# Three shared chunks behind the experts in place of two, in a fused attention and mixture-of-experts kernel

## The chip, the cores and the metric

One core of one Trainium2 chip runs the whole program. The metric is the device time of one execution in microseconds. The core has five engines that run their own instruction streams and meet only at semaphores: PE (matmuls), DVE (vector), ACT (scalar, activations), POOL (GpSimd) and SP, which here only issues DMAs.

## The reference

The input x is 4 sequences of 2048 tokens with 256 features (8192 tokens). Two residual layers follow each other:

```python
x = x + layernorm(attn(layernorm(x)))
x = x + layernorm(ffn(layernorm(x)))
```

`attn` mixes features and not tokens: per sequence and head (16 heads of 16 features), the distances between the rows of x @ Wqk give a 16x16 softmax that is applied to x @ Wv, and Wo follows. So one sequence needs a Gram matrix of x (256x256), a few small matrices made from it, and then one 256x256 matrix that every token is multiplied by.

`ffn` normalizes once more, sends each token to the 2 best of 7 experts (a router Wr, a capacity of 732 places per expert), and adds one shared expert that every token passes:

```python
out = routed + (silu(h @ W1s) * (h @ W3s)) @ W2s      # 256 -> 1024 -> 256
```

## The kernel before

**Groups and chunks.** The 8192 tokens are 16 groups of 512, four in each of four batches (a batch is a sequence). Feed-forward work comes in chunks: one group through the shared expert, or half of one expert's places (14 chunks). Every chunk runs through the same body of `FM` = 8 steps m. In each, PE computes two up projections into two PSUM banks (`up`, 12 matmuls of 512 columns, each product as three of high and low parts), ACT applies silu (L1063), DVE multiplies (L1738), ACT rounds to a high part (L1034), DVE takes the low part (L1714), and three steps later PE does the down projection (`down`, 12 matmuls of 256 columns) into banks 2 and 3. The first half of `up(m+1)` waits for silu of step m, the second half for the DVE multiply of step m. In the last two chunks before the experts, and in all after them, a second pair of banks makes both waits one step looser (`wide`).

**Three phases.** First come `FIRST` = 14 shared chunks with the whole attention and routing woven between them; then the 14 expert chunks; then the `HELD` = 2 shared chunks that were held back, with the final pass woven in.

**Places.** A step m has two places, 2m (behind `up`) and 2m+1 (behind `down` on PE, behind the low part on DVE); place numbers count from the first chunk, so chunk n has places 16n to 16n+15. A table written by hand, `schedule`, says at which place each small step of attention and routing is issued, on every engine that has a part in it. Batch b's steps are set by three origins: `X_AT` (per group q, 4 places apart: `x_stats`, `x_norm`, `x_high` on ACT, `x_part` on DVE, `x_gram` on PE), `M_AT` (the chain of small matrices) and `MIX_AT` (per group, 5 places apart: `o_mix` on PE, `o_stats` and `o_norm` on DVE, `o_apply` on ACT, `o_add`, `u_stats`, `u_norm` on DVE, two turns and the router on PE, `u_copy`). Each pair of groups is then routed: `r_top`, `r_next` on DVE, `u_count` on PE, `u_slot`, `u_place` on DVE. Engines take their streams strictly in order, so a step at place 66 on DVE stands ahead of everything at place 67.

**Waits that the prediction touches.** `x_high` waits for `x_norm`, `x_part` for `x_high`, `x_gram` for `x_part`; `u_count` waits for the second choice made by `r_next` (`r_oh`); `o_apply` waits for `o_norm`, which waits for POOL's power of -0.5.

**The final pass.** Fifteen groups (`GROUP[0..14]`) take the same steps at places `LAST_AT[g]` of the held chunks: DVE statistics (`last_stats`, `last_moments`, L1827 to L1841), a power on POOL (L913), the bias on DVE (L1845), the normalization on ACT in two halves (L1114, at places +3 and +4), and one POOL DMA that adds the group onto the output in DRAM (`last_sum`, L908), three groups later. The groups' expert sums are loaded by SP from `y_scratch` into 13 buffers. The last group (`CLOSE`) is finished from PSUM behind PE's last matmul: DVE adds it in two halves, takes statistics of all four tiles, waits for one power, normalizes, adds the residual and SP stores two halves.

```python
LAST0 = 9
HELD_PLACES = 2 * FM * HELD
LAST_AT = [LAST0 + g * (HELD_PLACES - LAST0 - 4) // (CLOSE - 1) for g in range(CLOSE)]
```

## Time and profile before

| what | value |
|---|---|
| median of 3 runs | 1089.29 us (1087.91 to 1089.88) |
| the profiled execution's own time | 1087.53 us |
| its span, first to last instruction | 1085.8 us |
| mean granted clock of PE | 0.993 |
| busy: PE, DVE, ACT, POOL | 1049.2, 656.1, 503.5, 390.0 us |
| the final pass's first statistics (place 9 of the held chunks) | 1017.77 us |
| DVE's first instruction behind PE's last matmul | 1075.90 us |

The span is what the rows are measured in; 1.7 us lie around it in the profiled execution. PE is busy for 97% of the span, but its busy time is modelled and overlaps from one matmul to the next, so that a group of rows is to be read by its starts. The clock column is the share of full speed (2.4 GHz) that PE was granted in a stretch.

### The profile page before, as it was taken

To read this page: it belongs to the slowest core of one execution; us is meant where nothing else is said; L and a number is where in the kernel's file an instruction comes from. 1 tells how busy PE (TensorE), PEld (TensorE's weight loads), DVE (VectorE), ACT (ScalarE), POOL (GpSimd) and SP (SyncE) were. 2 spreads that over 40 slices of the span, in tenths; PEclk is the share of its full clock that TensorE was granted. 3 is DMA by queue.
4 is the path that set the end of the run, shared out by engine and by line. 5 is a ranking of instruction groups with operands and counts; after the bars stand their busy time and mean duration, and the time that the engine had idled before them with its cause. 6 is when DMAs were issued, how large, how long until landed. Compare 5 with 4: busy or idle time off the path is not lost.

```text
span 1085.8 us, 19513 instructions
## 1 busy us (share of the span) xinstructions
PE 1049.2 (97%) x6863; PEld 958.5 (88%) x6863; DVE 656.1 (60%) x1714; ACT 503.5 (46%) x895; POOL 390.0 (36%) x347
## 2 busy tenths in 40 slices
PE   7998999999999999999989999999999999999995
PEld 6886888888888988889878899999999999999874
DVE  7768864677754578754786334545545463635686
ACT  4343344443434444443454334554546463645485
POOL 3112661114640114541116731344443343312386
PEclk9999999999999999999999999999999999999998
DMA  8322460242540223461134214524344342333699
GB/s 280 114 98 78 138 214 20 78 157 93 174 142 20 100 96 141 134 221 49 59 136 162 93 43 152 139 62 117 82 96 106 68 124 52 81 79 105 239 237 178
DMA packets 47229, 129.15 MB, mean 119 GB/s; under 512 B 10276, under 2 KB 17576, under 8 KB 47152
## 3 DMA queue, kind: packets, MB, share of 16 engines
q1 hardware_dynamic: 28656, 92.83, 25.1%
q0 software_dynamic: 18496, 35.35, 14.2%
q8 instruction: 43, 0.70, 0.3%
q14 instruction: 34, 0.28, 0.1%
HBM read 73.72 MB, written 54.40 MB: 118 GB/s over the span
## 4 chain that ended last, share of the span: by engine, by line
PE 82%; DVE 8%; POOL 3%; issue 3%; ACT 1%; DMA 1%; DVEq 0%; SPq 0%; POOLq 0%; ACTq 0%
PE bank L1140 25%; PE bank L1142 25%; PE bank L1141 25%; PE bank L1159 3%; POOL out_dram L908 2%; POOL sb_place_of L913 2%; DVE sb_act L1738 1%; PE bank L1266 1%; PE bank L1319 1%; DVE sb_act_lo L1714 1%; PE bank L1219 1%; DVE sb_stX L1431 1%; DVE sb_st L1431 1%; PE bank L1278 1%; ACT sb_ln_o L967 1%
## 5 line engine op out<-in xcount | busy, mean ns | idle before, releaser
L1140 PE MATMUL bank<-sb_h_hi,sb_wup_lo 128*128 128x512 f32 (+2 forms) x960 | 354.4, 369 | 5.3 <-DVE sb_act L1738 3.8
L1738 DVE TENSOR_TENSOR sb_act<-bank,sb_act 128x512 f32<-128x512 f32 (+2 forms) x240 | 148.6, 619 | 345.9 <-PE bank L1142 317.1
L1142 PE MATMUL bank<-sb_h_hi,sb_wup_hi 128*128 128x512 f32 (+2 forms) x960 | 350.0, 365 | 0.0
L1141 PE MATMUL bank<-sb_h_lo,sb_wup_hi 128*128 128x512 f32 (+2 forms) x960 | 349.6, 364 | 0.0
L1063 ACT ACTIVATE sb_act<-bank 128x512 f32<-128x512 f32 (+2 forms) x240 | 129.8, 541 | 354.6 <-PE bank L1142 328.9
L1140 PE MATMUL bank<-sb_wdn_hi,sb_act_lo 128*128 128x256 f32 (+1 forms) x848 | 246.5, 291 | 5.8 <-DVE sb_act_lo L1714 5.8
L1142 PE MATMUL bank<-sb_wdn_hi,sb_act_hi 128*128 128x256 f32 (+1 forms) x848 | 240.1, 283 | 0.0
L1141 PE MATMUL bank<-sb_wdn_lo,sb_act_hi 128*128 128x256 f32 (+1 forms) x848 | 239.9, 283 | 0.0
L1140 PEld LDWEIGHTS bank<-sb_h_hi,sb_wup_lo 128*128 128x128 f32 x960 | 180.5, 188 | 27.2 <-DVE sb_act L1738 6.4
L1142 PEld LDWEIGHTS bank<-sb_h_hi,sb_wup_hi 128*128 128x128 f32 x960 | 180.5, 188 | 22.5
L1141 PEld LDWEIGHTS bank<-sb_h_lo,sb_wup_hi 128*128 128x128 f32 x960 | 180.9, 188 | 17.0
L1140 PEld LDWEIGHTS bank<-sb_wdn_hi,sb_act_lo 128*128 128x128 f32 (+1 forms) x848 | 159.7, 188 | 11.6 <-DVE sb_act_lo L1714 6.9
L1714 DVE TENSOR_TENSOR sb_act_lo<-sb_act,sb_act_hi 128x512 fp32r<-128x512 f32 (+2 forms) x240 | 147.2, 613 | 36.1 <-ACT sb_act_hi L1034 34.8
L1141 PEld LDWEIGHTS bank<-sb_wdn_lo,sb_act_hi 128*128 128x128 f32 (+1 forms) x848 | 159.6, 188 | 3.3
L1142 PEld LDWEIGHTS bank<-sb_wdn_hi,sb_act_hi 128*128 128x128 f32 (+1 forms) x848 | 159.5, 188 | 0.0
L1034 ACT ACTIVATE sb_act_hi<-sb_act 128x512 fp32r<-128x512 f32 (+2 forms) x240 | 136.6, 569 | 0.3 <-DVE sb_act L1738 0.3
L864 POOL DMA_INDIRECT y_scratch<-sb_ysb,sb_scur x42 | 76.9, 1832 | 154.1 <-ACT sb_ysb L1052 87.8
L784 POOL TENSOR_TENSOR sb_rstdB<-sb_veB,sb_mhalf 128x4 f32<-128x4 f32 x16 | 19.0, 1187 | 218.1 <-DVE sb_veB L1557 218.1
L800 POOL DMA_INDIRECT sent_scratch<-sb_rows,sb_sendto x64 | 70.7, 1104 | 28.9 <-issue 19.9
L833 POOL DMA_INDIRECT sb_rows<-sent_scratch,sb_gcur x42 | 44.6, 1063 | 77.3 <-issue 52.5
L788 POOL TENSOR_TENSOR sb_rstd<-sb_ve,sb_mhalf 128x4 f32<-128x4 f32 x16 | 19.8, 1239 | 77.5 <-DVE sb_ve L1593 77.5
L967 ACT ACTIVATE sb_ln_o<-bank,sb_nbiasB,sb_rstdB 128x256 f32<-128x256 f32 x64 | 30.9, 563 | 27.5 <-DVE sb_nbiasB L1562 27.5
(265 smaller groups left out, 1240.6 us busy)
## 6 DMA issues: line engine op xcount, KB each, us to landing
sb_xin<-in_L_ffn_W_dram SPq DMA_DIRECT2D x28, 512.0 KB, 3.5
sb_x<-in_L_attn_x_dram SPq DMA_DIRECT2D x16, 512.0 KB, 3.7
out_dram<-sb_x SPq DMA_DIRECT2D x16, 512.0 KB, 3.5
sb_xin<-in_L_attn_x_dram SPq DMA_DIRECT2D x14, 512.0 KB, 5.1
sb_xin<-in_x_turned_dram SPq DMA_DIRECT2D x14, 512.0 KB, 3.9
y_scratch<-sb_ysb SPq DMA_DIRECT2D x14, 512.0 KB, 3.6
sb_xn<-in_L_ffn_W_dram SPq DMA_DIRECT2D x14, 512.0 KB, 3.9
hT_scratch<-sb_hr SPq DMA_DIRECT2D x12, 512.0 KB
```

The lines of the kernel that those rows point to most:

```text
L800: pool.indirect_dma_start(sent_d, bass.IndirectOffsetOnAxis(ap=sendto[:, q, t, c:c + 1], axis=0), u[q][:, t, :], None).then_inc(sent[q], 16)
L833: pool.indirect_dma_start(rows[0:w, part, t, :], None, sent_d, bass.IndirectOffsetOnAxis(ap=gcur[0:w, part, t:t + 1], axis=0)).then_inc(ga ...
L864: pool.indirect_dma_start(y_d, bass.IndirectOffsetOnAxis(ap=scur[0:w, par, part, t:t + 1], axis=0), ysb[0:w, part, t, :], None, compute_op ...
L967: ins = s.activation(ln_o[:, t, :], bank[o_bank(b, q) + t // 2][:, (t % 2) * D:(t % 2 + 1) * D], ACT.Identity, scale=rstdB[:, t:t + 1], bi ...
L1034: s.activation(act_hi[:, m % 4, 0:c.w], act[:, m % 3, 0:c.w], ACT.Copy).then_inc(ahi_ok, 1)
L1063: s.activation(act[:, m % 3, 0:c.w], a[:, 0:c.w], ACT.Silu).then_inc(silu_ok, 1)
L1140: t_.matmul(o, a_lo, b_hi, start=start, stop=False, skip_group_check=True)
L1141: t_.matmul(o, a_hi, b_lo, start=False, stop=False, skip_group_check=True)
L1142: return t_.matmul(o, a_hi, b_hi, start=False, stop=stop, skip_group_check=True)
L1159: ins = t_.matmul(bank[4 + k][:, o:c], a[:, k * P:(k + 1) * P], a[:, o:c], start=(q == 0 and t == 0), stop=(q == GB - 1 and t == GT - 1))
L1714: v.tensor_tensor(act_lo[:, m % 4, 0:c.w], act[:, m % 3, 0:c.w], act_hi[:, m % 4, 0:c.w].bitcast(F32), ALU.subtract).then_inc(alo_ok, 1)
L1738: v.tensor_tensor(act[:, m % 3, 0:c.w], bank[(4 if c.wide and m % 2 else 0) + 1][:, 0:c.w], act[:, m % 3, 0:c.w], ALU.mult).then_inc(act_o ...
```

## The change

`HELD` goes from 2 to 3, so 13 shared chunks stand before the experts and 3 behind them. Four things follow.

1. The woven steps of attention and routing must fit into 208 places, where there were 224. Batch 2 starts 6 places sooner (`X_AT` 66 for 72, `M_AT` 87 for 93, `MIX_AT` 101 for 109), batch 3 starts 16 places sooner (115 for 131, 136 for 152, 148 for 164). Batches 0 and 1 stay. The routing of batch 2 is drawn together: `r_top`, `r_next`, `u_count`, `u_slot` at places 31, 32, 33, 34 behind its origin for its second pair, where they were at 32, 34, 38, 39, and at 21, 21, 22, 23 for the first pair, where they were at 21, 21, 23, 24.
2. Batch 3's first group goes to `hT_scratch` in DRAM and back as the others do (one store and one load of 512 KB more), and 4 more DMAs write zeros into `y_scratch`.
3. The final pass has 48 places. `LAST_AT` runs from 9 to 40 where it ran from 9 to 28. A second group (14) is added from `ysb`; there are 12 buffers; the second last held chunk is loaded behind 11 of the loads.
4. The last group is finished in two halves: each half has its own statistics, moments and power (on POOL), the second is normalized and added to the residual in one DVE operation per tile, and the last `last_sum` stands behind both powers in POOL's stream.

```diff
     TB = N // P
     ST = -(-CAP // P)
     LASTW = CAP - (ST - 1) * P
-    HELD = 2
+    HELD = 3
     FIRST = NG - HELD
...
+
+        def by_memory(b, q):
+
+            return q > 0 or b == B - 1
+
+        def h_stores(b, q):
+            return b * H_LOADS + 16 * sum(by_memory(b, k) for k in range(q))
...
         LAST0 = 9
         CLOSE = NG - 1
         HELD_PLACES = 2 * FM * HELD
-        LAST_AT = [LAST0 + g * (HELD_PLACES - LAST0 - 4) // (CLOSE - 1) for g in range(CLOSE)]
-
-        GROUP = [*range(FIRST - 2), FIRST, FIRST - 2, FIRST - 1, CLOSE]
+        LAST_AT = [LAST0 + g * (HELD_PLACES - LAST0 - 8) // (CLOSE - 1) for g in range(CLOSE)]
+
+        GROUP = [*range(FIRST - 2), FIRST, FIRST - 2, FIRST - 1, FIRST + 1, CLOSE]
...
-                       (0, 1, 3, 3, 4, 4, 5, 6, 8, 8, 11, 12, 13, 13, 14, 14, 15),
+                       (0, 1, 2, 2, 3, 3, 4, 5, 6, 6, 9, 10, 11, 11, 12, 12, 13),
...
-        X_AT, M_AT, MIX_AT = (None, 14, 72, 131), (None, 34, 93, 152), (None, 46, 109, 164)
+        X_AT, M_AT, MIX_AT = (None, 14, 66, 115), (None, 34, 87, 136), (None, 46, 101, 148)
...
-            if b < B - 1:
+            if b == 1:
                 put_routing(b, MIX_AT[b], ((21, 21, 23, 24, 25), (32, 34, 38, 39, 40)), (27, 35, 43, 51), 2)
+            elif b == 2:
+                put_routing(b, MIX_AT[b], ((21, 21, 22, 23, 24), (31, 32, 33, 34, 35)), (26, 33, 40, 47), 2)
             else:
                 put_routing(b, MIX_AT[b], ((21, 21, 24, 25, 26), (31, 31, 34, 34, 35)), (27, 31, 36, 40), 1)
         for j in range(PIECES):
-            put(B - 1, 0, j, [("w_next", 157 if j < 3 else 181 + 2 * j), ("w_high", 182 + 2 * j), ("w_low", 184 + 2 * j)])
-        put(B - 1, 0, 0, [("indices", 200), ("zero_row", 170)])
+            put(B - 1, 0, j, [("w_next", 141 if j < 3 else 165 + 2 * j), ("w_high", 166 + 2 * j), ("w_low", 168 + 2 * j)])
+        put(B - 1, 0, 0, [("indices", 184), ("zero_row", 154)])
...
+            def last_rstd(g, cut, count):
+                pool.wait_ge(t_var, count)
+                v.tensor_tensor(t_scale[g % SLOTS][:, cut], t_ve[g % SLOTS][:, cut], mhalf[:, cut], ALU.pow).then_inc(t_rstd, 1)
+
+            for g in range(CLOSE):
+                last_rstd(g, slice(0, GT), g + 1)
                 if g == 0:
                     pool.wait_ge(t_idx, 1)
                     for k in range(2):
                         pool.wait_ge(x2_out[k], OPEN + 16 * (NG // 2))
                     pool.sem_inc(pool_go, 1)
-                if 3 <= g < CLOSE:
+                if g >= 3:
                     last_sum(g - 3)
-                if g == CLOSE - 1:
-                    for late in range(CLOSE - 3, CLOSE):
-                        last_sum(late)
+            for late in (CLOSE - 3, CLOSE - 2):
+                last_sum(late)
+            for h in range(2):
+                last_rstd(CLOSE, slice(2 * h, 2 * h + 2), NG + h)
+            last_sum(CLOSE - 1)
...
             def last_stats(g):
                 y = last_y[g % TY]
                 dve.wait_ge(t_y[g % TY], 16 * (g // TY + 1))
-                if g == CLOSE:
-                    last_half(g, 0)
-                elif GROUP[g] == FIRST:
-
-                    dve.wait_ge(y_sb, OPEN + NCH - HELD + 1)
-                    v.tensor_tensor(flat4(y), flat4(y), flat4(ysb[:, 0, :, :]), ALU.add).then_inc(t_sum, 1)
-                    dve.wait_ge(t_sum, 1)
+                if GROUP[g] in range(FIRST, CLOSE):
+
+                    h = GROUP[g] - FIRST
+                    dve.wait_ge(y_sb, OPEN + NCH - HELD + h + 1)
+                    v.tensor_tensor(flat4(y), flat4(y), flat4(ysb[:, h, :, :]), ALU.add).then_inc(t_sum, 1)
...
-            for t in range(GT // 2, GT):
-                ins = v.tensor_scalar(y[:, t, :], y[:, t, :], t_scale[CLOSE % SLOTS][:, t:t + 1], t_bias[CLOSE % SLOTS][:, t:t + 1],
-                                      ALU.mult, ALU.add)
-            ins.then_inc(t_sum, 1)
+            y, slot_of = last_y[CLOSE % TY], CLOSE % SLOTS
+            ch = Chain(dve, t_chain, 2 * CLOSE)
+
+            def close_sum(h):
+                dve.wait_ge((dn_half, dn_done)[h], (1, OPEN + NCH * FM)[h])
+                half = flat4(y[:, 2 * h:2 * h + 2, :])
+                v.tensor_tensor(half, half, bank[2 + h][:, :], ALU.add).then_inc(t_sum, 1)
+                dve.wait_ge(t_sum, HELD + h)
+                for t in (2 * h, 2 * h + 1):
+                    ins = v.bn_stats(st[:, t, :], y[:, t, :])
+                ch.link(ins)
+
+            def close_moments(h):
+                for t in (2 * h, 2 * h + 1):
+                    ins = v.bn_aggr(t_mv[slot_of][:, t, :], st[:, t, :])
+                ch.link(ins)
+                cut = slice(2 * h, 2 * h + 2)
+                v.tensor_scalar(t_ve[slot_of][:, cut], t_mv[slot_of][:, cut, 1], EPS, None, ALU.add).then_inc(t_var, 1)
+
+            dve.wait_ge(t_y[CLOSE % TY], 16 * (CLOSE // TY + 1))
+            close_sum(0)
+            close_moments(0)
+            close_sum(1)
+            dve.wait_ge(t_rstd, NG)
+            v.scalar_tensor_tensor(out=t_bias[slot_of][:, 0:2], in0=t_mv[slot_of][:, 0:2, 0], scalar=-1.0,
+                                   in1=t_scale[slot_of][:, 0:2], op0=ALU.mult, op1=ALU.mult).then_inc(t_nb, 1)
+            close_moments(1)
+            for t in (2, 3):
+                ins = v.tensor_scalar(y[:, t, :], y[:, t, :], t_mv[slot_of][:, t, 0:1], None, ALU.subtract)
+            ch.step(ins)
             dve.wait_ge(t_x, 16)
-            for h in (1, 0):
-                dve.wait_ge((t_act, t_sum)[h], (NG, HELD + 2)[h])
-                half = slice(2 * h, 2 * h + 2)
-                v.tensor_tensor(flat4(close_x[:, half, :]), flat4(close_x[:, half, :]), flat4(y[:, half, :]),
-                                ALU.add).then_inc(t_half, 1)
+            dve.wait_ge(t_act, NG)
+            v.tensor_tensor(flat4(close_x[:, 0:2, :]), flat4(close_x[:, 0:2, :]), flat4(y[:, 0:2, :]),
+                            ALU.add).then_inc(t_half, 1)
+            dve.wait_ge(t_rstd, NG + 1)
+            ch.settle()
+            for t in (2, 3):
+                ins = v.scalar_tensor_tensor(out=close_x[:, t, :], in0=y[:, t, :], scalar=t_scale[slot_of][:, t:t + 1],
+                                             in1=close_x[:, t, :], op0=ALU.mult, op1=ALU.add)
+            ins.then_inc(t_half, 1)
```

## Rows read from the trace of the kernel before

**Rows 1.** Busy time by stretch (start:end, length, busy us and count, clock, DMA share, GB/s)
```profile
53.90:644.60 590.70, 579.50 (x3667) 503.91 (x3660) 378.61 (x1043) 251.49 (x419) 206.13 (x186) 0.99 0.33 112
1019.90:1069.00 49.10, 44.59 (x257) 38.63 (x255) 43.39 (x170) 38.44 (x77) 34.10 (x26) 1.00 1.02 263
1069.00:1076.00 7.00, 5.55 (x30) 5.07 (x30) 3.57 (x8) 3.93 (x8) 5.89 (x5) 0.76 1.01 163
```

**Rows 2.** Timeline of PE, last two chunks: start, us, line, idle before, releaser
```profile
1047.50 0.36 PE L1140 MATMUL bank<-sb_wdn_hi,sb_act_lo 128*128 128x256 f32 x1 [2.48 <-DVE sb_act_lo L1714]
...
1067.27 0.38 PE L1140 MATMUL bank<-sb_wdn_hi,sb_act_lo 128*128 128x256 f32 x1 [1.27 <-DVE sb_act_lo L1714]
...
1070.32 0.39 PE L1140 MATMUL bank<-sb_wdn_hi,sb_act_lo 128*128 128x256 f32 x1 [2.08 <-DVE sb_act_lo L1714]
```

**Rows 3.** Timeline of DVE in a chunk with nothing beside it
```profile
615.13 0.69 DVE L1738 TENSOR_TENSOR sb_act<-bank,sb_act 128x512 f32<-128x512 f32 x1 [2.92 <-PE bank L1142]
...
619.35 0.69 DVE L1738 TENSOR_TENSOR sb_act<-bank,sb_act 128x512 f32<-128x512 f32 x1 [2.93 <-PE bank L1142]
```

**Rows 4.** Timeline of DVE in the last pass: one group's start and the next one's
```profile
1051.83 0.75 DVE L1827 BATCH_NORM_STATS2 sb_st<-sb_rows 128x6 f32<-128x256 f32 x2
...
1054.47 0.74 DVE L1827 BATCH_NORM_STATS2 sb_st<-sb_ysb 128x6 f32<-128x256 f32 x2
```

**Rows 5.** Timeline of ACT in the last pass
```profile
1046.30 1.06 ACT L1045 ACTIVATE sb_ysb<-bank 128x512 f32<-128x512 f32 x2
1047.25 2.08 ACT L1114 ACTIVATE sb_x<-sb_x,sb_place_of 128x256 f32<-128x256 f32 x4
```

**Rows 6.** Timeline of DVE at the close
```profile
1075.90 0.69 DVE L1813 TENSOR_TENSOR sb_xn<-sb_xn,bank 128x512 f32<-128x512 f32 x1 [0.93 <-PE bank L1142]
...
1080.30 1.29 DVE L1873 TENSOR_TENSOR sb_rows<-sb_rows,sb_xn 128x512 f32<-128x512 f32 x2
```

**Rows 7.** DMA issues of the end, KB each, median us to landing
```profile
out_dram<-sb_rows SPq DMA_DIRECT2D x2, 256.0 KB, 3.6
...
out_dram<-sb_ysb,sb_outidx POOLq DMA_INDIRECT x1, 6.1
```

**Rows 8.** Timeline of POOL, a power beside DVE and the close's
```profile
1057.60 2.35 POOL L913 TENSOR_TENSOR sb_place_of<-sb_place_of,sb_mhalf 128x4 f32<-128x4 f32 x1
...
1078.19 1.04 POOL L913 TENSOR_TENSOR sb_place_of<-sb_place_of,sb_mhalf 128x4 f32<-128x4 f32 x1 [0.92 <-DVE sb_place_of L1841]
```

**Rows 9.** Timeline of DVE, chunk 8 (places 130 to 137)
```profile
404.84 0.20 DVE L1634 TENSOR_REDUCE sb_best<-sb_lg 128x8 f32<-128x56 f32 x1
...
408.20 1.40 DVE L1431 BATCH_NORM_STATS2 sb_st<-sb_x 128x6 f32<-128x256 f32 x4
...
410.24 1.40 DVE L1431 BATCH_NORM_STATS2 sb_stX<-sb_xin 128x6 f32<-128x256 f32 x4
...
422.85 1.22 DVE L1568 TENSOR_TENSOR sb_wdn_hi<-sb_xn,sb_wdn_hi 128x1024 fp32r<-128x1024 f32 x1
```

**Rows 10.** Timeline of PE, a Gram step of batch 2
```profile
265.80 1.91 PE L1159 MATMUL bank<-sb_wdn_hi 128*128 128x512 f32 x8 [0.32 <-DVE sb_wdn_hi L1568]
```

**Rows 11.** Timeline of ACT before chunk 8: an o_apply
```profile
397.89 1.93 ACT L967 ACTIVATE sb_ln_o<-bank,sb_nbiasB,sb_rstdB 128x256 f32<-128x256 f32 x4 [1.78 <-DVE sb_nbiasB L1562]
```

**Rows 12.** Timeline of DVE, chunk 4 (places 68 to 71)
```profile
240.43 0.22 DVE L1638 TENSOR_TENSOR sb_oh<-sb_same,sb_first 128x56 bf16<-128x56 f32 x1
...
244.86 0.69 DVE L1738 TENSOR_TENSOR sb_act<-bank,sb_act 128x512 f32<-128x512 f32 x1 [0.83 <-PE bank L1142]
...
249.86 0.17 DVE L1680 CAST sb_sendto<-sb_pos 128x16 uint32<-128x16 f32 x1
```

**Rows 13.** Timeline of PE, chunk 4: a count, a turn
```profile
241.17 0.38 PE L1294 MATMUL bank<-sb_oh,sb_earlier 128*128 128x112 bf16 x4
...
251.44 0.60 PE L1266 MATMUL bank<-sb_ident,sb_early 128*128 128x128 f32 x4
```

**Rows 14.** Busy time by stretch, behind a stop of PE in batch 3
```profile
568.00:571.00 3.00, 2.04 (x10) 2.07 (x11) 2.62 (x10) 0.92 (x2) 0.00 (x0) 0.64 0.00 0
```

More of the change, by code:

```diff
@@ L173, in sandwich_kernel @@
         center = ysb[:, 1, 0:KC, :]
-        TY = 13
+        TY = 12
         SLOTS = 5
@@ L179, in sandwich_kernel @@
                   x2[:, 0, :, :], x2[:, 1, :, :], ln_o[:, :, :], by_tile(own[:, 0:GT * D]),
-                  by_tile(rowsf[:, 0:GT * D]), ysb[:, 1, :, :],
+                  by_tile(rowsf[:, 0:GT * D]),
                   hfull[:, :, :].rearrange("p k (t d) -> p (k t) d", d=D)]
@@ L676, in shared_places @@
                 for place in range(2 * FM):
-                    if place == (10 if n == 0 else 2) and j < GB - 1 and n + 1 < FIRST:
-                        load_h(b, j + 1)
+                    if place == (10 if n == 0 else 2) and n + 1 < FIRST and by_memory(*divmod(n + 1, GB)):
+                        load_h(*divmod(n + 1, GB))
                     if place == 2 * BEHIND + 2 and n > 0:
@@ L987, in step @@
                                      scale=gcol[:, 0:1], bias=bcol[:, 0:1]).then_inc(first_hi, 1)
-                    s.activation((hfull if q == 0 else hr)[:, k, :], bank[6 + k][:, :], ACT.Identity,
+                    s.activation((hr if by_memory(b, q) else hfull)[:, k, :], bank[6 + k][:, :], ACT.Identity,
                                  scale=gcol[:, k:k + 1], bias=bcol[:, k:k + 1]).then_inc(hT_ok, 1)
@@ L1008, in prep @@
                         act_e.wait_ge(hf_ok, c.x * 2 + 2)
-                    elif c.held or c.n % GB:
+                    elif c.held or c.loaded:
                         act_e.wait_ge(h_in, c.landed)
@@ L1808, in _ @@
                             ALU.mult).then_inc(t_idx, 1)
-            def last_half(g, h):
-                dve.wait_ge((dn_half, dn_done)[h], (1, OPEN + NCH * FM)[h])
-                half = flat4(last_y[g % TY][:, 2 * h:2 * h + 2, :])
-                v.tensor_tensor(half, half, bank[2 + h][:, :], ALU.add).then_inc(t_sum, 1)
-                dve.wait_ge(t_sum, HELD + h)
             def last_stats(g):
```

34 lines of the change are left out of this document (14 added, 20 removed).

## Prediction

> **What bounds the kernel now.** I read the busy times by stretch first, then PE's timeline for the waits in brackets, then DVE's and ACT's beside them. Of the 590.7 us in which attention is woven into 14 shared chunks, PE is busy for 579.5 [rows 1]; DVE has work for 64% of it. PE is the bound nearly everywhere, and DVE and ACT matter only where they make it stop. They do so in the last pass: the ten steps m from 1019.9 to 1069.0 took 49.1 us [rows 1]. PE stopped there and just behind for 2.48, 1.27 and 2.08 us, each time until DVE's low part was there [rows 2], and the clock stood at 0.76 over 1069 to 1076 [rows 1]. A step with nothing beside it takes 4.21 us [rows 3], so ten would have taken 42.1.
>
> **The held chunks: -7.0 us.** A group of the final pass costs DVE 2.64 us from its statistics to the next group's, of which one low part takes 0.6 [rows 4]: 2.05 us. It costs ACT 2.08 [rows 5]. The pitch is 19 places for 14 groups, at 2.1 us each 2.86 us; that is 72% of DVE, and its own two operations per step (1.2 of 4.21) are 29% more: with the low part of h, over 100%. ACT comes to 73% and 26%. Both fall behind, ACT takes `ysb` late (1.06 us, [rows 5]), and PE waits. After the change the pitch is 31 places for 14 groups, 4.66 us: DVE 44 + 29%, with a 1.2 us low part per chunk and two sums 80%; ACT 45 + 26% and one copy, 75%. The last group ends at place 44 of 48, so nothing of it stands in the last steps. There the last low part needs multiply, high part and low part, about 2.0 us behind `up(7)`; PE has two units of `down` (2.8 us) to do by then. So the 49.1 - 42.1 = 7.0 us go. The clock's share behind it (0.76 over 7 us with 5.55 busy, below 1 us) may go too; I leave it as one bound, -8.0. The other is -5.0, if PE still stops for 1 us at each of the two places where `ysb` is now taken.
>
> **The close: -0.4 us.** I count from DVE's second sum, 1075.90 [rows 6]. Before, the last store can go at 1081.6 [rows 6], lands 3.6 later [rows 7], and the span ends at +9.9. After: sum 0.72, statistics 0.9, bias 0.1, moments and the small add 0.4 give the second half's variance at +2.2; POOL takes it 0.25 later and needs 1.04 [rows 8]: +3.5. DVE's store goes at +4.4 and lands at +8.0. But `last_sum` of group 14 now stands behind that power: it starts at +3.7 and lands 6.1 later [rows 7], at +9.8, and some 0.4 us of waits follow. That row comes from a crowded queue; on an empty one I take 5.3 us, so +9.5. Ends: -1.4 (landing in 4.5) to +0.5 (6.3). The Trainium skill (GPSIMD Engine Reference, Specifications) says that GpSimd's SBUF interfaces are shared with VectorE and contend with DVE instructions that have two SBUF inputs. The trace agrees in kind: a power took 2.35 us beside a busy DVE where it takes 1.04 alone [rows 8]. The change puts the second power beside DVE's subtraction and its final two-input operations, so this rule speaks against it; it is a rival below.
>
> **The woven phase: +12.2 us.** Work is not added, it is pushed together: 16 places, one plain chunk, are gone from under it (that chunk's own PE time is only moved behind the experts). What counts is whether DVE, strictly in order, now makes PE stop. Costs: `x_stats` or `u_stats` 2.04 and the two choices 2.6 (3.36 with a low part and 0.15 of small ones), `x_part` or `x_low` 1.2 [rows 9]; a Gram step 1.8 on PE [rows 10]; `o_apply` 1.9 on ACT [rows 11]; `x_norm` and `u_norm`, four tiles like the statistics' 1.40 [rows 9], 1.3; `x_high`, 1024 columns on ACT like the 1.06 of [rows 5], 1.0. On PE, counted by starts, `up` is 2.8 and `down` 1.4 of the 4.21, a turn 0.35, the router 0.6. Five places are new:
>
> (1) Place 69, `u_count` of batch 1. Before, the choice was ready at 240.65 [rows 12] and the count began at 241.17 [rows 13]: 0.5 to spare. Now `x_stats` of batch 2 (2.04) stands ahead of it in place 66. Stop: 1.5.
>
> (2) Place 73, first Gram step of batch 2. It needs `x_part` of place 71. DVE's multiply of place 68, at 240.7 before, comes at 242.75; with 0.6, `u_stats` 2.04, 0.6 and `x_norm` 1.3 the next comes at 247.3. From there the old work took 244.86 to 250.0 [rows 12], 5.2, and now `x_stats` and `x_part` are in it: 255.7. PE, with its 1.5 us of delay, is there at 251.44 + 1.5 + 0.35 [rows 13] = 253.3. Stop: 2.5 (1.8 to 3.0).
>
> (3) Place 119. From a multiply on, DVE does `u_stats`, `x_norm` of batch 3 and the low part before `o_norm`: 4.55. Then ACT's `o_apply` 1.9 and `x_high` 1.0 stand ahead of silu, 0.5: 8.0. PE wants silu's result after a turn, `down`, `up`, the router and `down`: 6.6. Stop: 1.5.
>
> (4) Place 123, `u_count` in the place right behind `r_next`. DVE comes some 2.2 us late out of (3), then 0.6 and 2.6; PE has a turn, a Gram step, `down` and a turn, 4.0. Stop: 1.5.
>
> (5) Place 134, the second pair's count. DVE: multiply 0.6, `r_top` 1.5, `x_low` and `x_part` 2.4, low part 0.6, `r_next` 1.15: 6.25. PE: 4.2. Stop: 2.0. This one needs no lateness of DVE at all.
>
> Together 9.0 us. At smaller ones (batch 2's and 3's chain of small matrices, in which PE waits for DVE at every link, now starts with DVE late; Gram steps like the one that waited 0.32 [rows 10]) I take +2.2 net of the old ones that go; ends 0 and +4. A stop can also bring the clock down: behind one of 2.2 us the clock was 0.64 over 568 to 571 [rows 14], and half speed costs about 1 us each time; but it stayed at 1.00 through the 2.48 us stop [rows 1, 2]. Five stops of this size: +1.0, ends 0 and +3. PE never gets these back, as it is the bound. Batch 3's own steps keep their distances to each other and to the chunk borders. The extra store and load of one group, the four writes of zeros and the later loads stand on SP several places before anyone needs them: nothing; without that cover a transfer costs 3.6 to 6.1 us [rows 7]. On SP and POOL nothing queued behind is needed sooner.
>
> **Sum.** 12.2 - 7.0 - 0.4 = +4.8 us on the profiled execution: 1087.5 to 1092.3. It was 1.8 below the median, so the median goes from 1089.3 to 1094.1. 0.2% (2.2 us) is about what a measurement can tell from no change.
>
> **Rivals.**
>
> Faster: DVE is in time. If `x_stats`, `x_norm` and `x_part` of the next batch run in gaps of DVE, only (1) and (5) stay, which the order alone forces: +3.5. For it: 36% of DVE's time is free [rows 1]. Against it: the free time isn't in places 66 to 71 and 115 to 127; places 130 to 136 before were filled without a gap by the same mix at half the overlap. It decides when the whole woven phase loses less than 7.4 us, and gives 1089.3 - 7.4 + 3.5 = 1085.4. Chance 0.16.
>
> Same: stops (2) to (4) at half size, nothing for the clock and small ones at 2.0, so that 3.5 + 2.8 + 2.0 = 8.3 stands against 7.4. Time 1090. Chance 0.18.
>
> The last pass doesn't get its 7.0 us: both takes of `ysb` still stop PE for 1 us, as ACT does a half group ahead of each: -5.0, and 1096.1. For it: ACT's 75%. Chance 0.07.
>
> The clock: each of the five stops brings it down, +5 in place of +1; 1098. Against: the 2.48 us stop that left it alone [rows 2]. Chance 0.07.
>
> The contended power: 1.3 us more (2.35 for 1.04) on the chain to the last `last_sum`, 1095.4. Chance 0.05.
>
> The forecast: 0.47.
>
> So faster 0.16, same 0.18 and slower 0.66. Range: 1087 to 1098.5. It holds the forecast's own, 1091.5 to 1097 (the ends of the small stops and of the close), the rivals above it and the same-time one, and leaves out the centre of the faster one.
>
> **What would show it.** Right: in PE's timeline waits of 1.5 to 3 us before an L1294 (a count) near 241 and in chunks 7 and 8, and before an L1159 near 253; ACT's silu late near place 120; none over 1 us in the three held chunks, which take 34 us each; the last landing that of an L908-type DMA. The woven phase, from DVE's first multiply to the first expert chunk's, takes 590.7 - 33.7 + 12.2 = 569 us. Wrong: if those waits are below 1 us each, DVE had more slack than I give it; if the held chunks still take 37 us, the pitch was not what held them.

## The result, and the profile after

The changed kernel takes 1094.33 us (median of 5 runs, 1092.96 to 1096.52) against 1088.66 us of the kernel before on the same chip (5 runs, 1085.75 to 1089.88): a ratio of 1.0068, 95% interval 1.0051 to 1.0085. By the medians it is slower by 5.7 us, by the ratio by 7.4 (5.5 to 9.2); the prediction was slower by 4.8, at 1094.1.

The profiled execution took 1096.52 us, the slowest of the five, with a span of 1094.8 us against 1085.8. So the two traces differ by 9.0 us where the medians differ by 5.7. The terms below are those of the traces. Busy time by stretch, first the woven phase (from DVE's first multiply to that of the first expert chunk), then the last 15 steps of the held chunks, the steps to DVE's second closing sum, and two stretches behind stops of PE (start:end, length, busy us and count by engine, clock, DMA share, GB/s):

```profile
54.20:625.90 571.70, 548.54 (x3475) 475.45 (x3468) 367.65 (x1027) 240.22 (x400) 204.54 (x186) 0.99 0.34 116
1013.80:1077.00 63.20, 63.20 (x362) 55.34 (x362) 46.03 (x152) 46.35 (x88) 37.67 (x26) 1.00 0.76 154
1077.00:1082.60 5.60, 5.55 (x47) 5.34 (x46) 3.82 (x10) 0.63 (x1) 0.03 (x1) 1.00 0.81 151
...
105.00:112.00 7.00, 3.29 (x19) 2.63 (x18) 6.43 (x22) 0.60 (x1) 3.21 (x2) 1.00 0.21 85
431.00:438.00 7.00, 5.00 (x29) 4.00 (x29) 6.09 (x15) 1.67 (x3) 5.71 (x5) 0.77 0.54 166
```

The woven phase took 571.7 us. Before it took 590.7 with one chunk of 33.7 more [rows 1], so it is 14.7 us longer than 557.0. The held stage is as the prediction has it: PE is busy for the whole of 63.2 us, 15 steps at 4.21, with the clock at 1.00; in the last pass of before PE had 44.59 us busy in 49.1 [rows 1]. Between DVE's last multiply for the experts and its last one of all, the third held chunk adds 33.7 us and 7.0 are taken away (69.1 us before, 95.8 after). The rest lies behind that last multiply.

The five new stops of PE stand in its timeline (start, us, line, idle before, releaser):

```profile
242.75 0.37 PE L1311 MATMUL bank<-sb_oh,sb_earlier 128*128 128x112 bf16 x4 [1.41 <-DVE sb_oh L1655]
...
255.86 1.32 PE L1176 MATMUL bank<-sb_wdn_hi 128*128 128x512 f32 x5 [2.25 <-DVE sb_wdn_hi L1585]
...
392.65 0.50 PE L1157 MATMUL bank<-sb_h_hi,sb_wup_lo 128*128 128x512 f32 x1 [1.46 <-ACT sb_act L1080]
...
401.04 0.37 PE L1311 MATMUL bank<-sb_oh,sb_earlier 128*128 128x112 bf16 x4 [1.41 <-DVE sb_oh L1655]
...
434.39 0.37 PE L1311 MATMUL bank<-sb_oh,sb_earlier 128*128 128x112 bf16 x4 [2.00 <-DVE sb_oh L1655]
```

In the kernel before the count at 241.17 and the turn at 251.44 have no bracket [rows 13]. L1311, L1176, L1157 and L1080 of this kernel are L1294, L1159, L1140 and L1063 of the one before.

The close, in the timelines of DVE, POOL and SP and the DMA issues of the end:

```profile
1082.59 0.69 DVE L1874 TENSOR_TENSOR sb_hr<-sb_hr,bank 128x512 f32<-128x512 f32 x1
...
1084.45 0.17 DVE L1885 TENSOR_SCALAR sb_place_of<-sb_place_of 128x2 f32<-128x2 f32 x1
...
1085.49 0.69 DVE L1900 TENSOR_TENSOR sb_rows<-sb_rows,sb_hr 128x512 f32<-128x512 f32 x1 [0.35 <-ACT sb_hr L1146]
1086.10 0.87 DVE L1905 SCALAR_TENSOR_TENSOR sb_rows<-sb_hr,sb_place_of,sb_rows 128x256 f32<-128x256 f32 x2
```

```profile
1074.48 1.54 POOL L920 DMA_INDIRECT out_dram<-sb_xin,sb_outidx  x1 [0.31 <-issue]
1082.57 0.72 POOL L925 TENSOR_TENSOR sb_place_of<-sb_place_of,sb_mhalf 128x2 f32<-128x2 f32 x1 [6.55 <-DVE sb_place_of L1885]
1084.70 0.73 POOL L925 TENSOR_TENSOR sb_place_of<-sb_place_of,sb_mhalf 128x2 f32<-128x2 f32 x1 [1.41 <-DVE sb_place_of L1885]
1085.61 2.04 POOL L920 DMA_INDIRECT out_dram<-sb_xn,sb_outidx  x1 [0.18 <-issue]
```

```profile
1086.27 1.13 SPq L736 DMA_DIRECT2D out_dram<-sb_rows  x2
```

```profile
out_dram<-sb_rows SPq DMA_DIRECT2D x2, 256.0 KB, 2.1
...
out_dram<-sb_xn,sb_outidx POOLq DMA_INDIRECT x1, 7.5
```

DVE and the stores are done early: the stores land 2.1 us behind their issues, where they took 3.6 before [rows 7]. POOL stands idle for 6.55 us with group 14 ready, and issues its sum only at 1085.61. That transfer lands 7.5 us later, and the span ends 1.6 us behind it, 12.2 behind DVE's second sum where it was 9.9. In the trace of before the last thing to land was a store, and the span ended 0.5 us behind it.

### The profile page after: what moved, and what is told of

The parts are those of the page before. It is cut to its first block, busy times and chain, and to the rows that moved or that the text cites. A ratio compares the mean times of both kernels' runs of the same rounds, so it can differ in the third digit from the quotient of the medians.

```text
span 1094.8 us, 19526 instructions
## 1 busy us (share of the span) xinstructions
PE 1049.0 (96%) x6863; PEld 957.7 (87%) x6863; DVE 658.8 (60%) x1717; ACT 504.6 (46%) x895; POOL 390.2 (36%) x348
## 4 chain that ended last, share of the span: by engine, by line
PE 83%; DVE 11%; issue 2%; ACT 1%; DMA 1%; POOL 0%; POOLq 0%; SPq 0%; DVEq 0%; ACTq 0%
PE bank L1157 25%; PE bank L1159 25%; PE bank L1158 25%; PE bank L1176 3%; DVE sb_act L1755 1%; DVE sb_st L1448 1%; ACT sb_ln_o L984 1%; PE bank L1336 1%; DVE sb_act_lo L1731 1%; PE bank L1283 1%; PE bank L1236 1%; DVE sb_stX L1448 1%; DMA sb_ysb<-in_L_ffn_W2s_dram 1%; PE bank L1295 1%; DVE sb_early L1625 1%
## 5 line engine op out<-in xcount | busy, mean ns | idle before, releaser
L1157 PE MATMUL bank<-sb_h_hi,sb_wup_lo 128*128 128x512 f32 (+2 forms) x960 | 354.9, 370 | 7.2 <-DVE sb_act L1755 4.3
L1159 PE MATMUL bank<-sb_h_hi,sb_wup_hi 128*128 128x512 f32 (+2 forms) x960 | 350.1, 365 | 0.0
L1080 ACT ACTIVATE sb_act<-bank 128x512 f32<-128x512 f32 (+2 forms) x240 | 129.9, 541 | 348.8 <-PE bank L1159 334.0
L1157 PE MATMUL bank<-sb_wdn_hi,sb_act_lo 128*128 128x256 f32 (+1 forms) x848 | 244.8, 289 | 0.0
L1159 PE MATMUL bank<-sb_wdn_hi,sb_act_hi 128*128 128x256 f32 (+1 forms) x848 | 239.3, 282 | 0.0
L1157 PEld LDWEIGHTS bank<-sb_h_hi,sb_wup_lo 128*128 128x128 f32 x960 | 181.0, 189 | 29.1 <-DVE sb_act L1755 6.9
L1159 PEld LDWEIGHTS bank<-sb_h_hi,sb_wup_hi 128*128 128x128 f32 x960 | 180.6, 188 | 22.7
L1731 DVE TENSOR_TENSOR sb_act_lo<-sb_act,sb_act_hi 128x512 fp32r<-128x512 f32 (+2 forms) x240 | 147.4, 614 | 35.1 <-ACT sb_act_hi L1051 33.7
L1157 PEld LDWEIGHTS bank<-sb_wdn_hi,sb_act_lo 128*128 128x128 f32 (+1 forms) x848 | 158.6, 187 | 4.7 <-issue 1.0
L1159 PEld LDWEIGHTS bank<-sb_wdn_hi,sb_act_hi 128*128 128x128 f32 (+1 forms) x848 | 158.5, 187 | 0.0
L845 POOL DMA_INDIRECT sb_rows<-sent_scratch,sb_gcur x42 | 44.1, 1051 | 76.5 <-issue 51.7
```

The source lines that it names most:

```text
L845: pool.indirect_dma_start(rows[0:w, part, t, :], None, sent_d, bass.IndirectOffsetOnAxis(ap=gcur[0:w, part, t:t + 1], axis=0)).then_inc(ga ...
L1080: s.activation(act[:, m % 3, 0:c.w], a[:, 0:c.w], ACT.Silu).then_inc(silu_ok, 1)
L1157: t_.matmul(o, a_lo, b_hi, start=start, stop=False, skip_group_check=True)
L1159: return t_.matmul(o, a_hi, b_hi, start=False, stop=stop, skip_group_check=True)
L1731: v.tensor_tensor(act_lo[:, m % 4, 0:c.w], act[:, m % 3, 0:c.w], act_hi[:, m % 4, 0:c.w].bitcast(F32), ALU.subtract).then_inc(alo_ok, 1)
```

## The experiments

Each kernel was compared with the kernel before on its own chip; "against the changed kernel" is the difference of the two ratios times 1088 us. The changed kernel's own ratio is known to 1.9 us either way, and that enters every figure of the last column.

| kernel | median us (range) | ratio to before, 95% | against the changed kernel, us |
|---|---|---|---|
| changed kernel | 1094.33 (1092.96 to 1096.52) | 1.0068, 1.0051 to 1.0085 | |
| before, batch 2 at place 66 | 1091.59 (1090.66 to 1092.65) | 1.0038, 1.0025 to 1.0051 | |
| counts one place later | 1090.53 (1089.70 to 1091.49) | 1.0031, 1.0019 to 1.0042 | -4.0 |
| first Gram step one place later | 1092.16 (1091.01 to 1094.45) | 1.0054, 1.0039 to 1.0069 | -1.5 |
| denser last pass | 1103.89 (1102.79 to 1105.53) | 1.0151, 1.0138 to 1.0164 | +9.0 |
| group 14's sum ahead of both powers | 1089.73 (1087.25 to 1091.87) | 1.0018, 1.0008 to 1.0027 | -5.4 |
| group 14's sum between the powers | 1091.09 (1088.72 to 1095.00) | 1.0034, 1.0022 to 1.0045 | -3.7 |
| the close of before | 1089.24 (1088.87 to 1092.51) | 1.0021, 1.0012 to 1.0030 | -5.1 |
| three edits at once | 1084.45 (1083.20 to 1088.42) | 0.9983, 0.9971 to 0.9995 | -9.2 |
| and x_high, x_part later | 1092.08 (1091.50 to 1093.18) | 1.0044, 1.0031 to 1.0058 | -2.6 |
| and x_high alone later | 1084.02 (1082.39 to 1084.48) | 0.9963, 0.9949 to 0.9977 | -11.4 |

**Batch 2 begins six places earlier, alone, in the kernel before.**

```
-        X_AT, M_AT, MIX_AT = (None, 14, 72, 131), (None, 34, 93, 152), (None, 46, 109, 164)
+        X_AT, M_AT, MIX_AT = (None, 14, 66, 131), (None, 34, 93, 152), (None, 46, 109, 164)
```

> The kernel before, with only the four X steps of batch 2 started at place 66 in place of 72 (one origin of the table; M, MIX, two held chunks and everything else as before). Order theory (a step put ahead on DVE stops PE at named places): a stop of 1.4 us before the count of batch 1 near 242 us and one of 2.0 to 2.5 us before the first Gram step near 255 us, and the old waits of 0.3 us before the Gram steps near 265 and 275 gone: the woven phase +3 us, the whole 1091 to 1093 where before stands at 1088.7. Density theory (the phase loses because one chunk less covers the same work, wherever the steps stand): nothing is denser over the phase, so within 1 us of before.

It takes 1091.59 us, 4.1 more than before, within the 1091 to 1093 of the order theory. Stops (1) and (2) are there, at the size they have in the changed kernel:

```profile
241.77 0.37 PE L1294 MATMUL bank<-sb_oh,sb_earlier 128*128 128x112 bf16 x4 [1.43 <-DVE sb_oh L1638]
...
254.88 1.61 PE L1159 MATMUL bank<-sb_wdn_hi 128*128 128x512 f32 x5 [2.27 <-DVE sb_wdn_hi L1568]
```

No work was added or taken away. The origin moves the whole group of steps, the loads and PE's Gram steps with those of DVE and ACT. So the new order alone makes these stops, with no chunk less.

**The counts of batches 1 and 2 one place later.**

```
             if b == 1:
-                put_routing(b, MIX_AT[b], ((21, 21, 23, 24, 25), (32, 34, 38, 39, 40)), (27, 35, 43, 51), 2)
+                put_routing(b, MIX_AT[b], ((21, 21, 24, 24, 25), (32, 34, 38, 39, 40)), (27, 35, 43, 51), 2)
             elif b == 2:
-                put_routing(b, MIX_AT[b], ((21, 21, 22, 23, 24), (31, 32, 33, 34, 35)), (26, 33, 40, 47), 2)
+                put_routing(b, MIX_AT[b], ((21, 21, 23, 23, 24), (31, 32, 34, 34, 35)), (26, 33, 40, 47), 2)
```

> The changed kernel, with the counts of batch 1's first pair and of batch 2's both pairs one place later on PE (place 70, 124 and 135 for 69, 123 and 134; slot and place steps at the same place or as near behind); no step of DVE is earlier. Order theory: the three waits of 1.4, 1.4 and 2.0 us before a count shrink to 0, 0 and 0.6, so about 4 us less in the woven phase, of which a part may come back at the next step that DVE holds up (the Gram step near 255 above all, since DVE isn't any earlier): -2.5 to -4.5 us, 1090 to 1092. Density theory: DVE has the same work in the same places, so the lateness shows at the next wait in full: within 1 us of the changed kernel's 1094.3.

1090.53 us, 4.0 less than the changed kernel. PE's waits by releaser (us in total, times, longest):

```profile
PE bank L1157 <- DVE sb_act L1755: 6.3, 7, 2.8
PE bank L1157 <- ACT sb_act L1080: 2.8, 2, 1.5
PE bank L1176 <- DVE sb_wdn_hi L1585: 2.7, 2, 2.3
```

The same view of the changed kernel:

```profile
PE bank L1311 <- DVE sb_oh L1655: 4.8, 3, 2.0
PE bank L1157 <- DVE sb_act L1755: 4.3, 5, 2.7
PE bank L1157 <- ACT sb_act L1080: 2.8, 2, 1.5
PE bank L1176 <- DVE sb_wdn_hi L1585: 2.6, 2, 2.2
```

The waits for `sb_oh`, which is what a count needs, are gone. Some of them came back: those for DVE's multiply rise from 4.3 us (5 times) to 6.3 (7 times), since DVE is still late there. Some 3.1 us of all waits in the phase went, 23.2 to 20.1. One of them, 1.0 us at 112, isn't the edit's: it is absent wherever the clock fell at 107. So the edit takes away 2.1 us of waits in this trace. The clock, counted as below, lost 1.7 us where it lost 5.1, as it no longer fell near 256 and 433.

**The first Gram step of batch 2 one place later.**

```
-        GRAM_AT = (None, (9, 12, 16, 19), (7, 11, 15, 19), (7, 11, 15, 19))
+        GRAM_AT = (None, (9, 12, 16, 19), (8, 11, 15, 19), (7, 11, 15, 19))
```

> The changed kernel, with the first Gram step of batch 2 one place later (8 places behind X_AT[2] in place of 7, so place 74) and nothing else. Theory (the stop of 2.25 us before it is DVE's late x_part, and the half clock behind it hangs on that stop): the stop at 255.9 goes or falls below 0.5 us and the clock stays at 1.00 there, 2 to 3.5 us less than the changed kernel, 1091 to 1092.5. Rival (the stop is DVE's lateness as such, and moves with the Gram step or shows up at the next one): under 0.8 us less, 1093.5 to 1094.5, with a stop of over 1.5 us within the next 20 us.

Here both readings hold in part. The stop at 255.9 goes, but PE now stops at the same time before its next unit, for DVE's multiply that stands behind `x_part`:

```profile
256.42 0.50 PE L1157 MATMUL bank<-sb_h_hi,sb_wup_lo 128*128 128x512 f32 x1 [1.46 <-DVE sb_act L1755]
...
432.04 0.37 PE L1311 MATMUL bank<-sb_oh,sb_earlier 128*128 128x112 bf16 x4 [2.00 <-DVE sb_oh L1655]
```

2.25 us become 1.46, 0.8 less. The ratio gives 1.5 us less, but the two intervals overlap (1.0039 to 1.0069 against 1.0051 to 1.0085), so the times alone don't show a gain. The other row bears on the clock. It is stop (5), unchanged at 2.00 us. In the changed kernel the clock was 0.77 over 431 to 438 (the row above); here it stayed at 1.00, while it fell at 107, where it had not fallen in the changed kernel:

```profile
431.00:438.00 7.00, 5.96 (x45) 5.40 (x46) 3.69 (x11) 0.70 (x2) 4.99 (x5) 1.00 0.73 228
105.00:112.00 7.00, 4.35 (x18) 3.77 (x19) 6.43 (x22) 0.52 (x1) 3.37 (x3) 0.76 0.16 63
```

**A denser last pass in the changed kernel.** The 14 groups go to places 25 to 44, 19 places as in the kernel before, in place of 9 to 40.

```
-        LAST_AT = [LAST0 + g * (HELD_PLACES - LAST0 - 8) // (CLOSE - 1) for g in range(CLOSE)]
+        LAST_AT = [LAST0 + 16 + g * (HELD_PLACES - 16 - LAST0 - 4) // (CLOSE - 1) for g in range(CLOSE)]
```

> The changed kernel, with the final pass's 15 groups at the old pitch of 19 places for 14 groups, moved into the last two of the three held chunks (places 25 to 44; they were at 9 to 40). Pitch theory: DVE and ACT are over 100% filled again, PE stops again for a sum of 5 to 7 us in the last two chunks, ACT takes the held chunk's result late, and the last steps are held up: +6 to +8 us, 1100 to 1102. If three held chunks were enough by themselves (loads earlier, other buffers): within 1 us of the changed kernel.

1103.89 us: the direction is right, the size 9.0 us instead of 6 to 8. PE again waits for the low part, `sb_act_lo` (2.47, 1.14 and 1.71 us, where [rows 2] have 2.48, 1.27 and 2.08):

```profile
PE bank L1157 <- DVE sb_act_lo L1731: 5.3, 3, 2.5
```

From the first multiply of the expert chunks to the last multiply of all it takes 459.1 us, 8.1 more than in the changed kernel. The second sum comes another 1.4 later, and the span ends 13.2 instead of 12.2 behind it. (The last multiply itself is only 5.1 us later: this trace's woven phase is 2.6 us shorter, and it starts 0.4 sooner.) The way from one of DVE's multiplies to the next is that of the kernel before: six steps in order take 5.36, 4.54, 5.34, 4.22, 5.35 and 5.17 us there, from 1019.9 on, and 5.36, 4.53, 5.35, 4.22, 5.35 and 5.17 here, from 1031.8 on, where the changed kernel has 4.21 on average. So the pitch is what cost the 7.0 us. Two things make it more here: the clock fell at 1060, behind the first wait (1.7 us, not in the trace of before), and at the close group 14's sum is issued while the one before it is still on its way, and lands in 8.6 us. The waits that the profile shows, 2.48 and 1.27 us within the ten steps, are but a part of the 7.0; the rest is spread over matmuls that it counts as busy.

**Group 14's sum ahead of both closing powers, and between them.**

```
-            for late in (CLOSE - 3, CLOSE - 2):
+            for late in (CLOSE - 3, CLOSE - 2, CLOSE - 1):
                 last_sum(late)
             for h in range(2):
                 last_rstd(CLOSE, slice(2 * h, 2 * h + 2), NG + h)
-            last_sum(CLOSE - 1)
```

> The changed kernel, with POOL's last accumulating DMA (group 14) issued ahead of the two powers of the closing group instead of behind them. If that DMA ends the span, the stretch from DVE's last sum to the end falls from 12.2 to 8 or 9 us (the two stores, issued 4.5 us behind that sum, then land last): -3 to -4 us, 1090 to 1091.5. If its landing near the end was only beside the path: no change; and if the powers are now held up by the DMA's issue: up to +1.

1089.73 us, 5.4 less: a little more than expected. One line moved is worth 5.4 of the 7.4 us that the ratio gives for the change. POOL's timeline:

```profile
1076.29 1.54 POOL L920 DMA_INDIRECT out_dram<-sb_xn,sb_outidx  x1 [0.30 <-issue]
1082.54 0.72 POOL L925 TENSOR_TENSOR sb_place_of<-sb_place_of,sb_mhalf 128x2 f32<-128x2 f32 x1 [4.71 <-DVE sb_place_of L1884]
```

The second sum of DVE is at 1082.55 as in the changed kernel, and the span ends at 1089.5: 7.0 us behind it, not 12.2. The powers come when they came before; nothing was in the way of the earlier place.

In the second version the sum is issued behind the first power.

> The changed kernel, with group 14's sum (POOL's last accumulating transfer) between the two closing powers: it can start some 2.1 us earlier than in the changed kernel, at 1083.3 in place of 1085.4, and the second power waits behind its issue of 1.5 us, up to 0.3 us. Theory (the span ends a fixed 9.4 us behind the start of that transfer, 7.5 of landing and 1.8): about 2 us less than the changed kernel, ratio 1.0045 to 1.0055 to the kernel before. Rival (the landing of 7.5 us comes from sharing the DMA engines with the two last stores, whose time doesn't move): 0 to 1 us less, ratio 1.006 to 1.007. Rival (any place behind the first power is as good as ahead of it, since a queue of three such transfers drains first): all of the 4.6 us, ratio 1.002 to 1.003.

3.7 us less (the intervals of the two ratios don't overlap: 1.0022 to 1.0045 against 1.0051 to 1.0085), more than the first theory had and less than the third. The sum starts at 1082.51, and the span ends 7.9 us later, not 9.2 as in the changed kernel:

```profile
1082.51 1.59 POOL L920 DMA_INDIRECT out_dram<-sb_xn,sb_outidx  x1 [0.20 <-issue]
1083.72 1.15 POOL L925 TENSOR_TENSOR sb_place_of<-sb_place_of,sb_mhalf 128x2 f32<-128x2 f32 x1
```

```profile
out_dram<-sb_rows SPq DMA_DIRECT2D x2, 256.0 KB, 3.9
...
out_dram<-sb_xn,sb_outidx POOLq DMA_INDIRECT x1, 6.1
```

The fixed price is refuted: this transfer took 6.1 us, and the stores, issued 2.8 and 3.6 us behind it, 3.9 in place of 2.1. The last to land is now a store: the transfer lands at 1088.6, the stores at 1089.3 and 1089.9, and the span ends at 1090.4. So the stores lose by the transfer beside them, as the rival on sharing has it, though not in its size; that the transfer in turn loses by the stores in the changed kernel isn't shown.

**The close of before in the changed kernel**: one power for all four tiles, group 14's sum ahead of it. The edit puts back the loop `for g in range(NG)` of POOL, `last_half`, and the order (1, 0) of the stores.

> The changed kernel, with the last group closed as in the kernel before: one power over four tiles, group 14's sum ahead of it, second half of the output stored first. Compared with the changed kernel whose group 14 sum goes ahead of both powers (1089.7), it tells what the two halves are worth when nothing stands behind them. Theory (the sum behind the power costs the changed kernel its gain; the halves themselves shorten DVE's and POOL's chain by about 1.3 us): 1090.5 to 1092, so faster than the changed kernel by 2 to 4 and slower than the halves with the sum ahead by 1 to 2.5. Rival (the halves are worth nothing, as the last of the earlier sums ends the span either way): within 0.5 us of 1089.7. Rival (the two halves are what costs, whatever the order): under 1089.

1089.24 us, below the 1090.5 to 1092 of the theory and where its first rival has it. The ratio is 1.0012 to 1.0030; with two halves and the sum ahead it is 1.0008 to 1.0027. No difference can be told in the medians. In the two traces the span ends 8.4 us behind the second sum here and 7.0 there, so the halves shorten the chain by 1.4 us in one execution. The old close itself ends 1.5 us sooner here than the 9.9 of before; its stores land in 2.1 us and not 3.6. All of the change's loss at the close is the order of POOL's last instruction.

**Three edits at once**: counts, group 14's sum ahead, Gram step.

> The changed kernel with the three edits at once: the counts of batches 1 and 2 one place later, group 14's sum ahead of both closing powers, the first Gram step of batch 2 one place later. Theory (the three causes are independent, each place losing time by itself): the counts' -3.8, the close's -4.6 and -2.3 to -3 add up to about -11, so 1082 to 1085, faster than the kernel before by 0.2 to 0.5%. Rival (the stops share one lateness of DVE, which shows up at the next wait when one is taken away): at most -8, 1086 to 1088, no different from the kernel before.

1084.45 us, within the expected 1082 to 1085, and faster than the kernel before: 0.9983 (0.9971 to 0.9995). The three alone gave 4.0, 5.4 and 1.5, 10.9 in sum; together they give 9.2, and the difference is within what these figures can tell. In the traces nothing is lacking: without the wait at 112, which comes and goes with the clock, the phase's waits fall by 2.1 us with the counts, by 0.8 with the Gram step and by 3.0 with both. Each edit had already paid for DVE's lateness when alone: PE waits for DVE's multiply 7.7 us in all (8 times) where the changed kernel had 4.3. The profiled execution, at 1083.69, is one in which the clock never fell before the close.

**And batch 3's x_high and x_part one place later each.**

```
-                put(b, X_AT[b] + 4 * q, q, X_STEPS)
+                put(b, X_AT[b] + 4 * q, q, X_STEPS if b < 3 else (("x_stats", 0), ("x_norm", 3), ("x_high", 5), ("x_part", 6)))
```

> As the kernel with the three edits at once, and batch 3's x_high and x_part one place later each (5 and 6 places behind its start in place of 4 and 5), so that ACT has the silu of place 119 ahead of x_high. Theory (x_high stands ahead of silu and makes the stop of 1.46 us at 392.7): 1.0 to 1.5 us less than that kernel, 1081 to 1084. Rival (the silu is late because of o_apply and o_norm alone, or x_part's delay makes the Gram steps of batch 3 late): within 0.5 us of that kernel or slower by 1 to 2.

A miss: 1092.08 us, 7 more than the three edits. The stop that it was made for did shrink, but three others came, in PE's timeline:

```profile
389.61 0.50 PE L1156 MATMUL bank<-sb_h_hi,sb_wup_lo 128*128 128x512 f32 x1 [0.51 <-ACT sb_act L1079]
...
394.76 0.50 PE L1175 MATMUL bank<-sb_wdn_hi 128*128 128x512 f32 x1 [1.66 <-DVE sb_wdn_hi L1584]
...
411.50 0.60 PE L1175 MATMUL bank<-sb_wdn_lo 128*128 128x512 f32 x1 [4.59 <-DVE sb_wdn_lo L1584]
...
437.23 0.50 PE L1175 MATMUL bank<-sb_wdn_lo 128*128 128x512 f32 x1 [2.15 <-DVE sb_wdn_lo L1584]
```

`x_part` in place 6 is a single place ahead of the Gram step at 7, and on DVE other work now stands ahead of it: from the multiply at 403.96 it has low parts, `u_norm` and routing steps to do before it comes to `x_part` at 410.22.

**And of batch 3 x_high alone one place later**, `(("x_stats", 0), ("x_norm", 3), ("x_high", 5), ("x_part", 5))`.

> The kernel with the three edits at once, and of batch 3 only x_high one place later (5 places behind x_stats in place of 4, the same place as x_part), where the earlier attempt moved x_part too. Theory (x_high stands ahead of silu at place 119 and costs 1 us there; in the earlier attempt it was x_part's delay that made PE wait 4.6 us before a Gram step): the stop of 1.46 us at 389.8 falls to 0.5 and nothing takes its place, 1 us less than the three edits at once. Rival (DVE, in order, now waits for x_high in front of x_part and is late for the multiply behind it, four times): 1 to 4 us slower than the three edits at once, with waits for DVE's multiply of 0.5 to 1 us in chunks 7 and 8.

1084.02 us, ratio 0.9963 (0.9949 to 0.9977): 0.37% faster than the kernel before, 4.0 us by the ratio (2.6 by the medians), and the fastest of all here.

```profile
388.96 0.50 PE L1156 MATMUL bank<-sb_h_hi,sb_wup_lo 128*128 128x512 f32 x1 [0.51 <-ACT sb_act L1079]
```

Stop (3) is down from 1.46 to 0.51 and nothing came in its place. ACT now does silu at 388.30 and `x_high` (1.06 us) behind it, so `x_high` was the last thing ahead of silu. Against the three edits the ratio is 2.2 us better where the trace has 1.0; their intervals overlap, and the rest may be noise.

## Why the prediction was right, point by point

**The sign** was right, and so were the five stops and the held chunks. **The size** owes something to luck. The time is 1094.1 for 1094.33, but the difference of +4.8 stands against +5.7 in the medians and +5.5 to +9.2 by the ratio's interval, and in the traces, for which it was worked out, against +9.0. The terms, predicted and measured: woven phase +12.2 and +14.7; held chunks -7.0 and -7.0; from the last multiply to the second sum nothing of its own and -1.3; close -0.4 and +2.3; start of the phase 0 and +0.3. So the median agrees better than the working does: the profiled execution is 2.2 us above its median, the one of before 1.1 below. Of the 4.2 us that the terms miss, these two hide 3.3, and that is chance.

**The held chunks** hold exactly. PE doesn't wait between 1013.8 and 1077.0; neither take of `ysb` stops it, so the rival of 5.0 us is out. The denser pass brings the waits for the low part and the long steps back. The bound of -8.0, with the clock, is what happened in this execution: 5.6 us from the last multiply to the second sum where [rows 1, 2] had a stop of 2.08 and a clock of 0.76.

**The five stops** were 1.5, 2.5, 1.5, 1.5 and 2.0 us, sum 9.0; they are 1.41, 2.25, 1.46, 1.41 and 2.00, sum 8.5, each before the instruction named. The earlier start alone reproduces (1) and (2); moving the counts takes away (1), (4) and (5); moving `x_high` takes away most of (3). The rival with (2) to (4) at half size is out. The method was to lay DVE's own instructions end to end from one multiply to the next and compare with PE's time between the same places. It foretold DVE's multiplies at 242.75 and 247.3; they start at 242.75 and 247.29.

**The smaller stops** were put at +2.2 net, 0 to +4. All waits over 0.15 us in the phase come to 11.1 us before (13 of them) and 23.2 after (22): 12.1 more, less the 8.5 of the five leaves 3.6. New are 1.13 at 361 (a mix waits for ACT's `o_apply`), 0.91 and 0.60 at 301 and 313, 0.47 at 415, 0.63 at 448, and 1.01 at 112 (which is the clock's, see the last section); a wait of 1.05 at 313 went. That term was too small by 1.4.

**The clock** was put at +1.0, 0 to +3, as a price of stops. Cut into stretches of 4 us, each counted with its share below full speed times 4, the phase loses 3.4 us in the trace of before (near 108 and 568) and 5.1 in that of after (near 256, 433 and 549): +1.7. But which stops bring it is not fixed, see below; that a change with more stops of 2 us buys more chances of it is my guess. The rival that each of five stops brings it down is refuted: it fell behind two of them in the changed kernel.

Stops 12.1 and clock 1.7 make 13.8 of the 14.7; 0.9 is in waits too short to be listed, or not found. The same account holds for the others: phase less waits less clock is 542.5 us before (without the moved chunk), 543.4 in the changed kernel, 543.5 with the Gram step later, 544.1 with the counts later and 544.5 with three edits. So, to within 2 us, the work itself takes the same time throughout, and the loss lies in the stops and the clock behind them.

**The close** is the step that failed. The prediction read the order rightly: group 14's sum stands behind the second power. It started even sooner, +3.0 us behind the second sum and not +3.7, because the power over two columns took 0.73 us where four take 1.04 [rows 8]. But "on an empty one I take 5.3 us" for its landing was wrong: it took 7.5, outside the ends 4.5 and 6.3, and 1.6 more to the end of the span where 0.4 was allowed. No row had 5.3. The 6.1 of [rows 7] was taken as an upper estimate for a crowded queue, and it was no bound: it belongs to the fourth last of these transfers. The last two of before stand in the same view, among its DMA issues, and took 7.7 and 8.3 us:

```profile
out_dram<-sb_xin,sb_outidx POOLq DMA_INDIRECT x2, 8.0
```

The shortest of the 15 in that trace took 5.9 us, the median 7.0, the longest 9.2. An early issue in a full queue (9.1 us to landing with the sum ahead of the powers) is not paid for at the end; a late one in an empty queue is. A start at +3.0, 7.5 to the landing and 1.6 to the end make the +12.2 of the trace, 2.7 more than the +9.5 of the forecast. The same transfer issued 9.3 us earlier saves 5.4 us: that is what the order behind the powers lost.

**The contended power** did not occur: 0.72 and 0.73 us for the powers, with DVE's one-input subtraction beside the second. What was slow there was the issue of the last transfer, 2.04 us beside DVE's add and its two `scalar_tensor_tensor`, where it takes 1.54 with DVE idle. That is in line with the Trainium skill (GPSIMD Engine Reference, Specifications), which has GpSimd's SBUF interfaces contend with DVE instructions with two SBUF inputs; but an issue of 2.08 us stands at 1070.25 in this same trace too, and one at 1072.63 took 1.54 beside DVE's low part, which also has two SBUF inputs. So the cause of the slow issue is open.

**The rival "faster"** needed DVE in time for (2) to (4). It was not, but the room it pointed to was there: with 36% of DVE free, four small moves in the order turned a ratio of 1.0068 into 0.9963. One of them, the place of group 14's sum, has nothing to do with DVE.

## What to carry to other kernels

When work of one stage is pushed under fewer chunks of another, add up the in-order engine's instructions between two of its results that the bound engine waits for, and compare with what that engine has to do meanwhile; a mean busy share (64% here) doesn't show the stops. Then look at each stop for a consumer standing one place too early: a place later was nearly free here for the counts, the first Gram step and `x_high`, but not for `x_part`, so check how much other work of the producer stands between, or the stop moves on (1.46 of 2.25 us did) or grows (4.59). At the end of a kernel issue every transfer that is ready before the engine waits for anything else, and price its landing by the last transfers of its kind in the trace, one by one (7.7 and 8.3 us here), not by a single earlier row (6.1).
